# A scratch write of 256 columns on GpSimd ahead of each scatter in the experts' stage

## The chip, the cores and the metric

The kernel runs on one core of a Trainium2 chip. The metric is the device time of one execution in microseconds, the median of several runs; lower is better. The engines are named as the profile names them: PE is TensorE (PEld its weight loads), ACT is ScalarE, DVE is VectorE, POOL is GpSimd, SP is SyncE, which here only issues DMAs.

## What is computed

The input is 16 sequences of 512 tokens with 128 features. The first half is causal attention with 16 heads and ALiBi slopes, the second a mixture of 8 experts with the best 2 for each token, plus one shared expert. Each half ends with a residual sum and a layer norm. Cut to what matters here:

```python
x = layernorm(x + attention(x))                      # 8192 tokens x 128
logits = xf @ gate_w.T                               # 8 experts
probs = softmax(logits)
topw, topi = top_k(probs, 2)
topw = topw / (topw.sum(-1, keepdims=True) + 1e-20)
shared = (silu(xf @ shared_gate.T) * (xf @ shared_up.T)) @ shared_down.T
for e in range(8):                                   # hidden size 352
    y = (silu(xf @ gate[e].T) * (xf @ up[e].T)) @ down[e].T
    routed += y * comb[:, e]                         # comb: topw at topi, else 0
x = layernorm(x + shared + routed)
```

## The kernel before

The attention stage takes the first 790 us or so and is not touched. It leaves the normalised tokens in SBUF as `x1` (64 tiles of 128 tokens, each with an extra column for the token's number), the logits, and for each token the two places that it has in an order sorted by expert.

The experts' stage works on 64 tiles of 128 tokens in two chunks of 32 (`CHUNKS`, `CT`). For each chunk there is a DRAM buffer `x_sorted`, in which each token stands twice, under each of its experts, with groups padded to whole tiles: 72 tiles of 128 rows (`CSLOT`), 144 in all (`NSLOT`). The rows get there by **scatters of x**, one indirect DMA on GpSimd for each tile and choice (64 for a chunk, the helper `scatter`, line 336). Each sorted tile is loaded back by SyncE (`xs`, line 1219), transposed by TensorE (line 1299), multiplied with one expert's gate and up matrices (line 1277), passed through SiLU on ScalarE (line 1368) and the product on VectorE (line 1145), transposed again (line 1326), multiplied with the down matrix (line 1338), and copied by ScalarE from PSUM into one of four slots of `ys` (line 1393; the profile names the tile `e_raw`, as it lies in the space of the raw weights). From there a **scatter of y** on GpSimd (line 1432) writes it back in token order to the DRAM buffer `y_tokens`. Before ScalarE fills a slot of `ys` again, it waits until the scatter of four tiles back has landed (line 1390). Rows that only pad a group are left out by the bounds check.

The order of the work is a list of steps, written out by every engine: 24 steps of the shared expert on groups of four tiles (three steps a group, one for each part of the hidden size), 144 steps with one routed tile each, and 24 more of the shared expert. Each engine walks through the same steps and does its part, with fixed lags: at a step, TensorE does gate and up for the step's tile, the transpose of x for two steps ahead, that of the hidden tile for two back, and the down matrix for three back.

GpSimd's part of a step, in order, is this:

- At the first step of a shared group: the low part of the group's input (`group_x`, line 1420), for which TensorE waits before the group's gate two steps later (line 1267).
- At steps 10 to 23: one scatter of x for the second chunk (`scatter_next`), after a wait for the gate of the next step; two at every fourth step. That makes 18.
- At steps with a routed tile three back: the waits for the tile (`y_taken`) and for its row numbers (`row_ready`), then the scatter of y. In the first chunk `scatter_next` follows at 7 tiles of 10 (`PACE`), until the 64 scatters of x of the second chunk are done; the last of them follows the scatter of the 66th tile of y.
- The final norm: the inverse deviation as a power (`rstd`, line 1442) and the normalised tile (line 1447). For the first chunk's 32 tiles this comes at every second step of the second chunk (GpSimd's share at steps 104 to 166), for the second chunk's at every step from 175 on.

SyncE loads the first sorted tile of the second chunk only when all scatters of x have landed, and the first tile of `y_tokens` only when all of the chunk's scatters of y have landed; the loads of later tiles stand behind these waits in its queue.

Of the kernel before, what the change touches and what calls it, by code (L numbers as in the profile page):

```python
# [15 lines left out]
P = 128  # L16
# [317 lines left out]
def scatter(pool, keep, dram, c, t, n, done):  # L334

    pool.indirect_dma_start(out=dram["x_sorted"][c],
                            out_offset=bass.IndirectOffsetOnAxis(ap=keep["place_i"][n][:, c * CT + t:c * CT + t + 1], axis=0),
                            in_=keep["x1"][:, c * CT + t, :], in_offset=None).then_inc(done, 16)
# [626 lines left out]
STEPS = range(-LOAD, len(KINDS) - DOWN + NORM_LAG + 14)  # L965
MIX = ((PARTED + CSLOT + 4, 2), (PARTED + NSLOT + 5, 1))
SPLIT_AT = 8
PACE = 7


def tile_at(at):

    return (KINDS[at], WHICH[at]) if 0 <= at < len(KINDS) else (None, None)


def part_at(at, parts):

    kind, n = tile_at(at)
    if kind != SHARED:
        return None, None  # L980
    group, part = divmod(n, NCH)
    return (group, part) if part in parts else (None, None)


def mixed_at(step, lag):

    for chunk, (first, every) in enumerate(MIX):
        turn, rest = divmod(step - first, every)
        if rest == 0 and 0 <= turn - lag < CT:
            return chunk * CT + turn - lag  # L990
    return None


def experts(nc, io, dram, keep):

    with ExitStack() as ctx:
        def sb(name, shape, dt=F32):
            return ctx.enter_context(nc.sbuf_tensor("e_" + name, shape, dt))

        def ps(name):  # L1000
            return ctx.enter_context(nc.psum_tensor("e_" + name, [P, T], F32))

        def sem(name):
            return ctx.enter_context(nc.semaphore("e_" + name))
# [35 lines left out]
        var_eps = sb("var_eps", [P, TURN])  # L1040
        minus_half = sb("minus_half", [P, 1])
        rstd = sb("rstd", [P, TURN])

        gate_ps = [ps(f"gate_ps{n}") for n in range(2)]
        up_ps = [ps(f"up_ps{n}") for n in range(2)]
# [4 lines left out]
        names = """const_loaded experts_loaded const_set weight_kept weight_rest routed chosen prefix_ps prefix_kept placed places  # L1050
            exponents exponents_done weighted experts_set ids_set x_scattered row_ready x_ready xT_kept xT_rest gate_ready up_ready
            silu_done hid_done h_ready hT_kept y_ready y_taken half_set mix_half mixed stats_taken aggregated stats_ready
            rstd_ready result_ready group_kept group_rest group_ready group_taken""".split()
        S = {n: sem(n) for n in names}
        group_loaded = [sem(f"group_loaded{n}") for n in range(2)]
        xs_loaded = [sem(f"xs_loaded{n}") for n in range(TURN)]
# [6 lines left out]
        def split_at(step):  # L1063

            return divmod(step - SPLIT_AT, 2) if 0 <= step - SPLIT_AT < 2 * NE else None

        with nc.Block() as block:
# [327 lines left out]
            @block.gpsimd  # L1395
            def _(pool):
                pool.memset(minus_half[:], -0.5).then_inc(S["half_set"], 1)
                pool.wait_ge(S["half_set"], 1)
                scattered = [0]

                def scatter_next():

                    choice, t = divmod(scattered[0], CT)
                    if choice == 2:
                        return
                    if t == 0:
                        if choice == 0:
                            pool.wait_ge(S["places"], 1)
                        else:
                            pool.wait_ge(S["x_scattered"], 16 * CT)  # L1410
                        pool.tensor_copy(x1[:, CT:NTILE, C:RW], keep["ids"][:, choice, CT:NTILE].unsqueeze(2)).then_inc(S["ids_set"], 1)
                        pool.wait_ge(S["ids_set"], choice + 1)
                    scatter(pool, keep, dram, 1, t, choice, S["x_scattered"])
                    scattered[0] += 1

                for step in STEPS:
                    group, part = part_at(step + TURNED, (0,))
                    if group is not None:
                        pool.wait_ge(S["group_kept"], group + 1)
                        pool.tensor_tensor(group_x[group % 2][:, 1, :], group_in[group % 2][:],  # L1420
                                           group_x[group % 2][:, 0, :].bitcast(F32), ALU.subtract).then_inc(S["group_rest"], 1)
                    if 10 <= step < PARTED:
                        pool.wait_ge(S["gate_ready"], step + 1)
                        scatter_next()
                        if step % 4 == 3:
                            scatter_next()
                    kind, n = tile_at(step + DOWN)
                    if kind == ROUTED:
                        chunk, slot = n // CSLOT, n % TURN
                        pool.wait_ge(S["y_taken"], n + 1)  # L1430
                        pool.wait_ge(S["row_ready"], n + 1)
                        pool.indirect_dma_start(out=dram["y_tokens"][chunk],  # L1432
                                                out_offset=bass.IndirectOffsetOnAxis(ap=row_i[:, n:n + 1], axis=0),
                                                in_=ys[:, slot, :], in_offset=None, bounds_check=2 * CT * P - 1,
                                                oob_is_err=False).then_inc(y_stored[chunk][slot], 16)
                        if chunk == 0 and (n + 1) * PACE // 10 > n * PACE // 10:
                            scatter_next()
                    tile = mixed_at(step, 2)
                    if tile is not None:
                        slot = tile % TURN  # L1440
                        pool.wait_ge(S["stats_ready"], tile + 1)
                        pool.tensor_tensor(rstd[:, slot:slot + 1], var_eps[:, slot:slot + 1], minus_half[:],  # L1442
                                           ALU.pow).then_inc(S["rstd_ready"], 1)
                        if tile >= TURN:
                            pool.wait_ge(out_stored[slot], 16 * (tile // TURN))
                        pool.wait_ge(S["rstd_ready"], tile + 1)
                        pool.tensor_scalar(result[:, slot, :], mixed[:, slot, :], mean_var[:, slot, 0:1],  # L1447
                                           rstd[:, slot:slot + 1], ALU.subtract, ALU.mult).then_inc(S["result_ready"], 1)
# [30 lines left out]
def build(nc, io):  # L1479

    dram = {"out": io["out"],
            "x_sorted": [nc.dram_tensor(f"x_sorted{c}", (CSLOT * P, RW), F32).ap() for c in range(CHUNKS)],
            "x1T": nc.dram_tensor("x1T_all", (B, P, T), F32).ap(),
            "y_tokens": [nc.dram_tensor(f"y_tokens{c}", (2 * CT * P, C), F32).ap() for c in range(CHUNKS)]}
    with ExitStack() as ctx:
        def sb(name, shape, dt=F32):
            return ctx.enter_context(nc.sbuf_tensor(name, shape, dt))

        keep = {"x1": sb("x1_all", [P, NTILE, RW]), "logits": sb("logits", [P, NTILE, NE]), "rank": sb("rank", [P, NE]),
                "ids": sb("ids", [P, 2, NTILE]), "before": sb("before", [P, P], BF16), "onesb": sb("onesb", [P, P], BF16),  # L1490
                "top": [sb("best", [P, NTILE]), sb("second", [P, NTILE])], "keyed": sb("keyed", [P, CT, NE]),
                "top_key": sb("top_key", [P, CT]), "one": [sb(f"one{n}", [P, CT, NE]) for n in range(2)],
                "others": sb("others", [P, CT, NE]), "chosen": sb("chosen", [P, CT, NE], BF16),
                "counts": sb("counts", [P, NE, CT]), "running": sb("running", [P, NE, CT]),
                "ones_f": sb("ones_f", [P, NE * CT]), "first": sb("first", [P, NE]), "group_n": sb("group_n", [P, NE]),
                "group_i": sb("group_i", [P, NE], I32), "padded": sb("padded", [P, NE]), "shift": sb("place_shift", [P, NE]),
                "ends": sb("ends", [P, CHUNKS, NE]), "place": sb("place", [P, CT, NE]), "place_f": sb("place_f", [P, CT]),
                "place_i": [sb("place_best", [P, NTILE], I32), sb("place_second", [P, NTILE], I32)]}
        keep |= {"shared_in": sb("shared_in", [P, 2, F]), "shared_down": sb("shared_down", [P, NCH, C])}
        attention(nc, io, dram, keep)  # L1500
        experts(nc, io, dram, keep)
# [14 lines left out]
```

## Time and profile before

| | |
|---|---|
| median of 3 timed runs | 1244.45 us (1243.96 to 1244.94) |
| profiled execution, first to last instruction | 1288.1 us; the page has no other time for it |
| TensorE busy | 1067.3 us, 83% |
| VectorE, ScalarE, GpSimd busy | 829.4, 695.8, 703.8 us |
| attention | about 0 to 790 us |
| first shared stage (steps 0 to 23) | about 790 to 831 us |
| first chunk (72 tiles) | about 831 to 1037 us |
| second chunk (72 tiles) | about 1037 to 1199 us |
| second shared stage, then the last results | 1199 to 1254, then to 1288 us |

The profile is one execution of the program, taken by the hardware profiler. A timeline row has the start, the length, engine, line, operation, output and inputs; in square brackets stands how long the engine had been idle before, and what released it. "issue" there is time in which the engine waited for nothing that the profile shows, "remote" an unknown releaser. The time of a DMA instruction on GpSimd is that of writing its descriptors; the data move later.

### The profile page before, as it was taken

Reading aid. Unit: us, or ns where it says so; the run is one execution under the profiler, and the core shown is the slowest. Engines: PE = TensorE matmul, PEld = TensorE weight load, DVE = VectorE, ACT = ScalarE, POOL = GpSimd, SP = SyncE. Lnnn points to the kernel's source line nnn. Section 1 sums busy time; section 2 is a strip of 40 time slices with the busy share of each in tenths; the row PEclk is TensorE's granted clock in tenths of the full one; section 3 lists DMA queues with packets and bytes.
Section 4 is the critical chain, followed back from the end, with each engine's and each line's share of the span. In section 5 each row is a group of like instructions: output and inputs, shape, how many; then the busy total and the mean of one; then the engine's idle time right before and its main releaser. Section 6 shows DMA issues by size and latency. Waiting matters only on the chain. (4 is left out here: it accounts for less than half of the span.)

```text
span 1288.1 us, 28760 instructions
## 1 busy us (share of the span) xinstructions
PE 1067.3 (83%) x9396; PEld 725.3 (56%) x9396; DVE 829.4 (64%) x2134; ACT 695.8 (54%) x1513; POOL 703.8 (55%) x1166
## 2 busy tenths in 40 slices
PE   1677898898989988999888849988878879999990
PEld 0333444444444443444444328877777779999880
DVE  2667888898888988988887137732222226655594
ACT  1016666666666664766667714454444446666430
POOL 0004554454545543777677722655555537888686
PEclk9958999999999998999999858999999889999995
DMA  5624534344344442553341224222222123333242
GB/s 93 75 40 68 82 65 77 79 70 82 68 77 84 69 77 46 88 109 88 75 107 27 69 62 171 60 60 61 62 60 59 52 56 104 113 108 106 76 120 73
DMA packets 124769, 100.48 MB, mean 78 GB/s; under 512 B 19952, under 2 KB 115574, under 8 KB 124178
## 3 DMA queue, kind: packets, MB, share of 16 engines
q1 hardware_dynamic: 114786, 76.55, 29.6%
q0 software_dynamic: 8704, 16.87, 4.1%
q10 hardware_dynamic: 1136, 5.23, 1.2%
q8 instruction: 81, 1.33, 0.4%
q14 instruction: 62, 0.51, 0.2%
HBM read 37.88 MB, written 35.79 MB: 57 GB/s over the span
## 5 line engine op out<-in xcount | busy, mean ns | idle before, releaser
L709 ACT ACTIVATE probs<-scores 128x512 f32<-128x512 f32 x640 | 346.7, 599 | 112.5 <-PE scores L622 105.4
L772 POOL TENSOR_SCALAR_AFFINE_SELECT probs<-probs 128x256 f32<-128x256 f32 (+1 forms) x640 | 234.5, 380 | 248.6 <-ACT probs L709 238.5
L599 PE MATMUL maxed<-kstack,qstack 52*128 52x128 bf16 (+3 forms) x1152 | 223.2, 299 | 71.0 <-DMA kstack<-parts 38.3
L622 PE MATMUL scores<-qstack,kstack 64*128 64x512 bf16 (+3 forms) x1024 | 236.1, 304 | 40.9 <-ACT probs L709 17.4
L1145 DVE TENSOR_TENSOR e_hid<-e_gate,e_up_ps 128x352 f32<-128x352 f32 (+2 forms) x192 | 107.6, 561 | 234.5 <-ACT e_gate L1368 149.1
L919 DVE TENSOR_REDUCE maxA<-maxed 128x4 f32<-128x512 f32 x256 | 165.6, 684 | 81.1 <-PE maxed L606 80.4
L1432 POOL DMA_INDIRECT y_tokens<-e_raw,e_row_i x144 | 145.6, 1011 | 120.2 <-ACT e_raw L1393 81.2
L638 PE MATMUL pv<-probs,vaug 128*32 128x512 f32 (+3 forms) x2048 | 197.7, 460 | 2.9 <-POOL probs L772 2.9
L919 DVE TENSOR_REDUCE maxB<-maxed 128x4 f32<-128x512 f32 x256 | 162.4, 682 | 4.9 <-PE maxed L606 4.9
L604 PE MATMUL maxed<-causal,halves 64*128 64x256 bf16 (+1 forms) x640 | 159.7, 261 | 0.0
L622 PEld LDWEIGHTS scores<-qstack,kstack 64*128 64x128 bf16 x1024 | 75.7, 94 | 145.8 <-ACT probs L709 81.5
L1368 ACT ACTIVATE e_gate<-e_gate_ps 128x352 f32<-128x352 f32 (+2 forms) x192 | 95.5, 498 | 98.4 <-PE e_gate_ps L1267 57.9
L606 PE MATMUL maxed<-causal,halves 64*128 64x192 bf16 (+1 forms) x640 | 143.6, 228 | 0.0
L1338 PE MATMUL e_y_ps<-e_w_down,e_hT 128*128 (+1 forms) x864 | 128.0, 286 | 15.8 <-ACT e_raw L1393 13.0
L599 PEld LDWEIGHTS maxed<-kstack,qstack 52*128 52x128 bf16 x1152 | 74.8, 95 | 91.4 <-issue 41.0
L1338 PEld LDWEIGHTS e_y_ps<-e_w_down,e_hT 128*128 128x128 f32 (+1 forms) x864 | 112.8, 199 | 21.5 <-issue 21.2
L1277 PE MATMUL e_gate_ps<-e_w_in,e_xT 128*128 x432 | 108.9, 361 | 1.8 <-DVE e_w_in L1078 1.8
L1277 PE MATMUL e_up_ps<-e_w_in,e_xT 128*128 x432 | 96.0, 332 | 0.0
L1326 PE MATMUL e_h_ps<-e_ident,e_hid 128*128 128x128 f32 x432 | 73.9, 282 | 20.3 <-ACT e_hT L1380 14.7
L1380 ACT ACTIVATE e_hT<-e_h_ps 128x384 f32<-128x384 f32 x144 | 71.0, 493 | 24.5 <-PE e_h_ps L1326 17.6
L919 DVE TENSOR_REDUCE maxC<-maxed 128x4 f32<-128x512 f32 x128 | 82.5, 684 | 1.0 <-PE maxed L606 0.4
L1277 PEld LDWEIGHTS e_up_ps<-e_w_in,e_xT 128*128 128x128 f32 x432 | 76.6, 195 | 0.0
(160 smaller groups left out, 1824.1 us busy)
## 6 DMA issues: line engine op xcount, KB each, us to landing
qstack<-parts SPq DMA_DIRECT2D x192, 64.0 KB
kstack<-parts SPq DMA_DIRECT2D x192, 64.0 KB
x_sorted<-zeros SPq DMA_DIRECT2D x16, 580.5 KB
e_xs<-x_sorted SPq DMA_DIRECT2D x144, 64.5 KB
e_raw<-y_tokens SPq DMA_DIRECT2D x64, 128.0 KB
xin<-in_x SPq DMA_DIRECT2D x16, 256.0 KB, 3.1
xres<-in_x SPq DMA_DIRECT2D x16, 256.0 KB
x1T_all<-ynT SPq DMA_DIRECT2D x16, 256.0 KB
```

The source lines that it names most:

```text
L599: pe.matmul(bank[:, at:at + (k1 - k0) * P], q[rows, slot, i * P:(i + 1) * P], ks[rows, slot, k0 * P:k1 * P], start=first, stop=False, skip ...
L604: pe.matmul(bank[:, at:at + wide], halves[rows, 0, :], causal[rows, 0:wide], start=False, stop=False, skip_group_check=True)
L606: pe.matmul(bank[:, at + ROWS:at + wide], halves[rows, 1, :], causal[rows, 2 * P:P + ROWS + wide], start=False, stop=True, skip_group_chec ...
L622: last = pe.matmul(scores[st.at(0, SEQ_UNITS, n) % SB][:, col:col + width], ks[rows, slot, kt * P:(kt + 1) * P], q[rows, slot, kt * P:T], ...
L638: last = pe.matmul(pv[hh * VW:(hh + 1) * VW, kt * P:T], vaug[st.par(off)][:, kt, g * QUAD + hh, :], probs[g % 2][:, at * T + col:at * T + ...
L709: act.activation(probs[g % 2][:, u * T:(u + 1) * T], scores[st.at(0, SEQ_UNITS, UNITS * g + u) % SB][:], ACT.Exp).then_inc(S["exp_done"], 1)
L772: pool.affine_select(out=view, in_=view, compare_op=ALU.is_ge, fill=0.0, base=0, pattern=pattern, channel_multiplier=-1).then_inc(S["maske ...
L919: dve.tensor_reduce(out.rearrange("p a b -> p (a b)"), maxed[st.at(max_stage(n), MAXB, n) % MB][:].rearrange("p (j t) -> p j t", t=P), AX. ...
L1145: dve.tensor_tensor(hid[step % len(hid)][rows, 0:cols], gate[step % 2][rows, 0:cols], up_ps[step % 2][rows, 0:cols], ALU.mult).then_inc(S[ ...
L1277: last = pe.matmul(bank[:, 0:F], xT[n % len(xT)][:, x_part, :], w_in[:, e, w, w_part, :].rearrange("p a f -> p (a f)"), start=m == 0, stop ...
L1338: last = pe.matmul(y_ps[:, 0:C], hT[n % 2][0:fw, j * P:(j + 1) * P], w_down[0:fw, e, j, :].rearrange("p a c -> p (a c)"), start=j == 0, st ...
L1432: pool.indirect_dma_start(out=dram["y_tokens"][chunk], out_offset=bass.IndirectOffsetOnAxis(ap=row_i[:, n:n + 1], axis=0), in_=ys[:, slot, ...
```

## The change

A tile `pause` of 128 partitions x 256 float is added and a semaphore `paused`. A helper writes zeros into the tile, with a wait for the write before, and is called ahead of every scatter of x in this stage and ahead of the two waits of every scatter of y. Nothing reads the tile. The scatters of x for the first chunk, which run in the attention stage, stay as they are.

```diff
+PAUSE = 256
...
+        pause = sb("pause", [P, PAUSE])
...
-                scattered = [0]
+                scattered, pauses = [0], [0]
+
+                def take_pause():
+
+                    if pauses[0]:
+                        pool.wait_ge(S["paused"], pauses[0])
+                    pool.memset(pause[:], 0.0).then_inc(S["paused"], 1)
+                    pauses[0] += 1
...
                         pool.wait_ge(S["ids_set"], choice + 1)
+                    take_pause()
                     scatter(pool, keep, dram, 1, t, choice, S["x_scattered"])
                     scattered[0] += 1
...
                     if kind == ROUTED:
                         chunk, slot = n // CSLOT, n % TURN
+                        take_pause()
                         pool.wait_ge(S["y_taken"], n + 1)
                         pool.wait_ge(S["row_ready"], n + 1)
                         pool.indirect_dma_start(out=dram["y_tokens"][chunk],
```

## Rows read from the trace of the kernel before

**Rows 1.** The head of the profile's page.

```profile
span 1288.1 us, 28760 instructions
```

**Rows 2.** Stage table: busy us (instructions) of each engine, clock, DMA share, GB/s.

```profile
801.00:832.00 31.00, 29.20 (x181) 25.16 (x180) 26.50 (x48) 14.57 (x31) 23.79 (x23) 1.00 0.23 65
840.50:1032.80 192.30, 155.65 (x1056) 144.24 (x1054) 52.61 (x198) 91.00 (x263) 108.96 (x112) 0.95 0.21 60
1068.00:1197.00 129.00, 129.00 (x988) 127.07 (x987) 76.82 (x331) 88.79 (x247) 107.50 (x124) 1.00 0.38 107
```

**Rows 3.** Groups by form on POOL: busy us, mean ns, idle us before, releasers.

```profile
L738 POOL MEMSET ones_f<- 128x256 f32 x1 | 0.3, 317 | 0.0
```

**Rows 4.** Timeline of POOL in the first chunk: start us, us, instruction, idle before.

```profile
840.57 1.00 POOL L1432 DMA_INDIRECT y_tokens<-e_raw,e_row_i  x1 [9.10 <-ACT e_raw L1393]
...
947.52 0.98 POOL L1432 DMA_INDIRECT y_tokens<-e_raw,e_row_i  x1 [1.88 <-ACT e_raw L1393]
948.81 0.97 POOL L336 DMA_INDIRECT x_sorted<-x_all,place_second  x1 [0.31 <-issue]
950.08 0.99 POOL L1432 DMA_INDIRECT y_tokens<-e_raw,e_row_i  x1 [0.30 <-issue]
951.37 0.96 POOL L336 DMA_INDIRECT x_sorted<-x_all,place_second  x1 [0.30 <-issue]
...
1032.83 0.96 POOL L336 DMA_INDIRECT x_sorted<-x_all,place_second  x1 [0.30 <-issue]
```

**Rows 5.** Timeline of PE and ACT in the first chunk and at its end.

```profile
953.99 0.27 PE L1299 MATMUL e_x_ps<-e_ident,e_xs 128*128 128x128 f32 x1
...
956.17 0.28 ACT L1372 ACTIVATE e_xT<-e_x_ps 128x128 fp32r<-128x128 f32 x1 [2.39 <-remote]
...
1036.97 0.47 PE L1299 MATMUL e_x_ps<-e_ident,e_xs 128*128 128x128 f32 x1 [4.65 <-DMA e_xs<-x_sorted]
```

**Rows 6.** Waits from 840 to 1020 us: us in total, times, longest.

```profile
ACT e_raw L1393 <- remote: 25.9, 15, 2.2
ACT e_raw L1393 <- PE e_y_ps L1338: 12.0, 28, 1.4
```

**Rows 7.** Waits from 1060 to 1200 us.

```profile
ACT e_raw L1393 <- PE e_y_ps L1338: 14.4, 38, 0.9
```

**Rows 8.** Timeline of POOL in the second chunk.

```profile
1068.95 0.61 POOL L1442 TENSOR_TENSOR e_rstd<-e_var_eps,e_minus_half 128x1 f32<-128x1 f32 x1
...
1173.05 0.98 POOL L1432 DMA_INDIRECT y_tokens<-e_raw,e_row_i  x1 [0.30 <-issue]
1174.04 0.60 POOL L1442 TENSOR_TENSOR e_rstd<-e_var_eps,e_minus_half 128x1 f32<-128x1 f32 x1
1174.82 0.80 POOL L1447 TENSOR_SCALAR e_raw<-e_raw,e_mean_var,e_rstd 128x128 f32<-128x128 f32 x1 [0.18 <-POOL e_rstd L1442]
1175.80 1.10 POOL L1432 DMA_INDIRECT y_tokens<-e_raw,e_row_i  x1 [0.18 <-issue]
1177.20 0.99 POOL L1432 DMA_INDIRECT y_tokens<-e_raw,e_row_i  x1 [0.30 <-issue]
...
1197.70 1.28 POOL L1420 TENSOR_TENSOR e_group_x<-e_group_in,e_group_x 128x512 fp32r<-128x512 f32 x1
```

**Rows 9.** Timeline of POOL and PE in the first shared stage.

```profile
807.39 1.30 POOL L1420 TENSOR_TENSOR e_group_x<-e_group_in,e_group_x 128x512 fp32r<-128x512 f32 x1
808.85 1.09 POOL L336 DMA_INDIRECT x_sorted<-x_all,place_best  x1 [0.17 <-issue]
...
808.94 0.94 PE L1267 MATMUL e_gate_ps<-e_group_x,e_w_in 128*128 128x512 f32 x3
...
815.78 0.94 PE L1267 MATMUL e_gate_ps<-e_group_x,e_w_in 128*128 128x512 f32 x3
```

**Rows 10.** Timeline of PE at the start of the second shared stage.

```profile
1199.13 0.93 PE L1267 MATMUL e_gate_ps<-e_group_x,e_w_in 128*128 128x512 f32 x3 [0.54 <-POOL e_group_x L1420]
```

More of the change, by code:

```diff
@@ L1052, in experts @@
             silu_done hid_done h_ready hT_kept y_ready y_taken half_set mix_half mixed stats_taken aggregated stats_ready
-            rstd_ready result_ready group_kept group_rest group_ready group_taken""".split()
+            rstd_ready result_ready paused group_kept group_rest group_ready group_taken""".split()
         S = {n: sem(n) for n in names}
```

## The prediction, made before the change was run

> **What bounds the kernel now.** I read the page first, for the span and the busy shares, then the stage table, then the groups of GpSimd by form, then GpSimd's own timeline in two stages, and last the waits. No engine bounds the whole: the span is 1288.1 us [rows 1], and the change touches only the last third, where TensorE is busy 29.2 of 31, then 155.65 of 192.3, then all of 129 us [rows 2]. What matters there is GpSimd, although it is busy only 57% of the long middle stretch.
>
> A scatter costs GpSimd more than its bar. Where scatters queue up, one starts 1.29 us after the y scatter at 947.52 and the next 1.27 us after that [rows 4]: 0.97 to 0.99 us of work and 0.30 us in which it is idle on "issue". Behind a computing instruction the gap is 0.18 us and the bar 1.10 us [rows 8], or 1.09 us for a scatter of x [rows 9]: again 1.28 us from the end of what came before. So 1.28 us is the price of a scatter, and none of it overlaps the instruction ahead of it.
>
> In the first routed chunk GpSimd has 66 scatters of y and 46 of x between 840.57 and 1032.83 us [rows 4], 112 in all and 111 intervals, 192.3 us. At 1.28 us they need 142.1 us; TensorE, at 128.75 us for 62 tiles in the second chunk [rows 8], would need 65 x 2.08 = 135 us. Neither explains 192.3. The other 50 us are stalls of this kind: TensorE's transpose into e_x_ps starts at 953.99 and is 0.27 us long, ScalarE's copy of it waits for nothing else by the code, and starts at 956.17, after 2.39 us of idle time that the trace puts down to "remote" [rows 5]. There are 15 such waits ahead of e_raw alone, 25.9 us together [rows 6]. The one shown comes a few microseconds behind the scatters of rows 4, which follow each other at 1.28 us. In the second chunk, where a scatter comes every 2.08 us on average, e_raw waits for TensorE's own matmul, 0.9 us at most [rows 7].
>
> In the second chunk GpSimd is full. Two tiles cost it two scatters, the power (rstd) and the normalised tile: from the rstd at 1068.95 to the subtraction for group 8 at 1197.70 there are 31 such pairs of steps in 128.75 us, 4.15 us each [rows 8], and by price 2 x 1.28 + 0.61 + 0.18 + 0.80 = 4.15 us. TensorE already waits 0.54 us for that subtraction [rows 10]. GpSimd has no slack in this stage.
>
> **How profile and median stand.** The sum is to be made against the profiled execution, whose span alone is 1288.1 us; the median of three timed runs is 1244.45 us, 43.65 us less. So something in the profiled execution takes longer than in a timed one. The one thing in the trace that has this size and no cause in the code is the 50.2 us of stalls just worked out. Without them the span would be 1288.1 - 50.2 = 1237.9 us, and 6.5 us around it make the median. I take it that the stalls belong to the recording. The Trainium skill's page "Runtime: NRT & Kernel Launch", section "The ~15µs preamble/postamble breakdown", has a profile's total some 6.2 us above the time reported without one; by it 37.5 us of the difference would be left over, so this case does not fit that figure. The page "NOTIFIC — the notification-queue block", section 7.1, says that its internal pipeline holds back the producer rather than lose a record, which would be a way for recording to slow TensorE; no run here shows it yet.
>
> **The change part by part.** It adds 208 pauses (64 ahead of scatters of x in this stage, 144 ahead of those of y), each a memset of 128 x 256 float on GpSimd, and a semaphore. The trace of before has that very shape once: 0.317 us [rows 3]. A pause starts about 0.01 us behind a scatter (rstd does, at 1174.04 [rows 8]), and puts the scatter behind it into the form that follows a computing instruction: 0.01 + 0.32 + 0.18 + 1.10 = 1.61 us instead of 1.28, so 0.33 us more. The wait on the pause before is for an instruction that lies a whole scatter back: nothing. Bounds: below, 0.20 us, if scatter and memset overlapped by the 0.12 us in which the two gaps differ (0.30 and 0.18); above, 0.43 us, if the 0.11 us by which the bar grows came on top. I take 0.33, because the sums of gap and bar agree in rows 8 and 9.
>
> Shared stage, 18 pauses. GpSimd's subtraction for a group runs 807.39 to 808.69, and TensorE starts the group's gate at 808.94 [rows 9]: 0.25 us of cover. Four scatters stand between two subtractions; with pauses such a turn is 4 x 1.61 + 1.45 = 7.9 us against the 6.84 us from one group's gate to the next (808.94 to 815.78). The first shown slips by 0.6 us behind TensorE, the next by about 1.0 more, then there are only three scatters and it recovers. Together +1.6 us, 0 to 3.
>
> First chunk, 65 tiles with 46 scatters of x. The pause stands ahead of the wait for e_raw, so where GpSimd waits for a tile it is hidden: the waits before scatters are over 1 us at both ends of the stage, and 9.1 us before the first [rows 4]. Further in, GpSimd has 1.7 x 1.61 = 2.74 us of work per tile against TensorE's 2.08, so it falls behind at once, and with four slots of ys ScalarE soon waits for the stores and all go at GpSimd's pace: 111 x 1.60 = 177.6 us. Against a timed run without the stalls (142.1) this is +35.5 us. Against the profile (192.3) it is -14.7. What is late next is the same in both: TensorE's transpose of the second chunk's first tile waits for the last scatter of x and its load, from 1032.83 to 1036.97 [rows 4, 5], and this tail of 4.1 us stays.
>
> Second chunk. GpSimd's pair of steps goes from 4.15 to 4.15 + 2 x 0.335 = 4.82 us against TensorE's 4.16. Queued behind each pause are the scatter, the rstd, the result and in the end the subtraction for group 8, for which TensorE waits already. 31 x 0.67 = +20.8 us, all of it on the path; the four slots can only delay when it is seen. Behind that subtraction four scatters remain (1.3 us at most if nothing covered them), at the pace of the shared tiles, and the last 32 results have no scatters; I count nothing.
>
> The sum for a timed run: 1244.45 + 1.6 + 35.5 + 20.8 = 1302.4 us. For the profiled execution: 1288.1 + 1.6 - 14.7 + 20.8 = 1295.8 us, if the pauses, which set scatters 1.6 us apart, also end the stalls.
>
> **The rivals.**
> The stalls are real. Then timed runs have them too, and the change takes them away as in the profile: 1244.45 + 1.6 - 14.7 + 20.8 = 1252.2 us. For it: nothing in the trace marks the stalls as the recorder's. Against it: the 43.65 us would then have to lie elsewhere, and I find no place for them. Half of them real would give about 1277.
>
> The pauses win. The stalls are real and a pause costs less than I take. In the first chunk the gain is 50.2 us less 111 pauses, in the second the loss is 62 pauses; with some 5 in the shared stage that count, the balance is zero at 50.2 / 178 = 0.28 us a pause. At the lower bound of 0.20 us it is -50.2 + 22.2 + 12.4 + 1.0 = -14.6, that is 1229.8 us. Against it: rows 8 and 9 leave no room for an overlap, and the memset's bar alone is 0.317.
>
> No slack, but less of it than I think. If a scatter takes less time in an unrecorded run, say 1.20 us, TensorE bounds both stages before the change, and part of the pauses is covered: 111 x 1.52 - 135 = +34 and 31 x (4.64 - 4.16) = +15, with 1 us for the shared stage 1294 us. This, and 0.43 us a pause on the other side (+76 us, 1320), are the ends of my forecast's own range; I narrow it to 1288 to 1310.
>
> The pauses are hidden everywhere, or are not carried out: 1244 us. It needs GpSimd to have 0.33 us to spare per scatter in an unrecorded run, that is a scatter under 0.95 us, less than the bar alone.
>
> **How the numbers follow.** My forecast has 0.66, half of the stalls real 0.08, all of them real 0.16, the pauses win 0.07, hidden 0.03. The predicted time is the likeliest's, 1302. The range of 8 in 10 has to take in the case of the real stalls: 1249 to 1310, with 1288 to 1310 for the forecast alone. What a measurement of this kernel can tell from no change is about 0.2%, 2.5 us. Faster by more than that: 0.08 (the winning pauses and a little of the real stalls); within it: 0.03; slower by more: 0.89.
>
> **What would show it.** In the profile of the changed kernel: memsets of 0.32 us with a 0.18 us gap behind them; scatters in the first chunk 1.60 us apart and never at 1.28; idle time of ScalarE on "remote" gone, and "DMA y_tokens" in its place as ScalarE waits for a slot; the pairs in the second chunk 4.8 us long with TensorE idle for some 0.3 us a tile; a span of about 1296 us. If the time is then above the span, or just under it, the stalls were the recorder's; if the time is some 40 us under the span as before, the missing time lies elsewhere and the first rival holds. I would be wrong if GpSimd's pair in the second chunk stayed under 4.3 us, or if scatters at 1.6 us still left ScalarE on "remote".

## The result, and the profile after

The changed kernel takes 1284.72 us (median of 4 runs, 1279.14 to 1287.53), the kernel before 1244.2 us (4 runs, 1239.36 to 1244.94, among them the three known before). The ratio is 1.0325, 95% interval 1.0292 to 1.0358: 40.5 us slower. I had forecast 57.9 us slower. The ratios and intervals here and below are those of the comparison as recorded; they leave the slow executions out and are not exactly the quotients of the medians beside them.

First the head of the page of the changed kernel, and the pauses from its groups by form.

```profile
span 1285.8 us, 28982 instructions
...
PE 1071.4 (83%) x9396; PEld 725.5 (56%) x9396; DVE 834.5 (65%) x2134; ACT 695.4 (54%) x1513; POOL 768.5 (60%) x1374
...
L1407 POOL MEMSET e_pause<- 128x256 f32 x208 | 69.7, 335 | 0.3
```

All 208 pauses are there. This span is 2.3 us *below* that of rows 1, although the kernel takes 40.5 us more, and that was the first thing to clear up. This profiled execution has a time beside it, 1287.53 us, 1.7 us above its span. For the profile before the page gave none.

Now the stage table (stretch, its length, busy us of PE, PEld, DVE, ACT and POOL, then clock, DMA share, GB/s): first chunk from the first to the last scatter of its burst (192.3 us in rows 2), then the second chunk from the first rstd to the subtraction for group 8 (129.0 us in rows 2).

```profile
850.50:1016.30 165.80, 145.34 (x1055) 139.08 (x1053) 52.21 (x199) 91.70 (x264) 145.10 (x223) 0.98 0.25 69
1051.90:1193.00 141.10, 134.09 (x990) 129.03 (x988) 76.90 (x329) 89.04 (x248) 125.03 (x185) 0.99 0.35 98
```

The timeline of POOL in the changed kernel: the ends of the first chunk and four neighbours inside it.

```profile
850.50 1.00 POOL L1443 DMA_INDIRECT y_tokens<-e_raw,e_row_i  x1 [7.54 <-ACT e_raw L1395]
...
943.50 0.34 POOL L1407 MEMSET e_pause<- 128x256 f32 x1
944.00 0.96 POOL L336 DMA_INDIRECT x_sorted<-x_all,place_second  x1 [0.17 <-issue]
944.95 0.34 POOL L1407 MEMSET e_pause<- 128x256 f32 x1
945.46 0.99 POOL L1443 DMA_INDIRECT y_tokens<-e_raw,e_row_i  x1 [0.17 <-issue]
...
1016.34 0.96 POOL L336 DMA_INDIRECT x_sorted<-x_all,place_second  x1 [0.17 <-issue]
```

The scatters at 944.00 and 945.46 are 1.46 us apart, where I had said 1.60 and where two in rows 4 are 1.27 to 1.29 apart. What ScalarE's copy waits for in this stretch is now a slot of `ys` (rows 6 had "remote" there):

```profile
ACT e_raw L1395 <- DMA y_tokens<-e_raw,e_row_i: 46.7, 37, 4.0
...
ACT e_raw L1395 <- PE e_y_ps L1340: 6.7, 29, 0.9
```

And the chain of waits that ended last, for some microseconds of the first chunk (start, us, and what the time went to; a DMA's time ends with its landing):

```profile
946.44 0.33 POOL e_pause L1407
946.93 0.96 POOL x_sorted L336
947.89 0.33 POOL e_pause L1407
948.22 0.17 issue
948.39 3.45 DMA y_tokens<-e_raw,e_row_i
...
951.92 0.29 ACT e_raw L1395
```

The pauses stand on the chain itself; then comes a scatter of y with its landing, then ScalarE, which waited for that slot.

### The profile page after: what moved, and what is told of

Same layout as the page of the kernel before. It is cut to its first block and busy times, and to the rows that moved or that the text cites. A ratio compares the mean times of both kernels' runs of the same rounds, so it can differ in the third digit from the quotient of the medians.

```text
span 1285.8 us, 28982 instructions
## 1 busy us (share of the span) xinstructions
PE 1071.4 (83%) x9396; PEld 725.5 (56%) x9396; DVE 834.5 (65%) x2134; ACT 695.4 (54%) x1513; POOL 768.5 (60%) x1374
## 5 line engine op out<-in xcount | busy, mean ns | idle before, releaser
L599 PE MATMUL maxed<-kstack,qstack 52*128 52x128 bf16 (+3 forms) x1152 | 226.1, 301 | 71.7 <-DMA kstack<-parts 36.4
L622 PE MATMUL scores<-qstack,kstack 64*128 64x512 bf16 (+3 forms) x1024 | 238.9, 307 | 44.8 <-DMA qstack<-mparts 17.7
L1395 ACT ACTIVATE e_raw<-e_y_ps 128x128 f32<-128x128 f32 x144 | 39.9, 277 | 90.5 <-DMA y_tokens<-e_raw,e_row_i 68.9
L606 PEld LDWEIGHTS maxed<-causal,halves 64*128 64x128 bf16 x640 | 64.0, 101 | 25.8 <-issue 7.6
```

What stands on the lines that cost most here:

```text
L599: pe.matmul(bank[:, at:at + (k1 - k0) * P], q[rows, slot, i * P:(i + 1) * P], ks[rows, slot, k0 * P:k1 * P], start=first, stop=False, skip ...
L606: pe.matmul(bank[:, at + ROWS:at + wide], halves[rows, 1, :], causal[rows, 2 * P:P + ROWS + wide], start=False, stop=True, skip_group_chec ...
L622: last = pe.matmul(scores[st.at(0, SEQ_UNITS, n) % SB][:, col:col + width], ks[rows, slot, kt * P:(kt + 1) * P], q[rows, slot, kt * P:T], ...
```

## The experiments

Three questions were open: whether the 50 us of stalls belong to the recording, what one pause costs, and how the 40.5 us divide between the two chunks. Each comparison is with the kernel before on the same chip. To compare stages I read the same marks in every trace: first subtraction of group_x, first scatter of y, last scatter of x, transpose of the 73rd tile, first rstd, subtraction for group 8, end. The stretch ahead of the first mark, attention, which no edit touches, varies from 771 to 788 us from run to run, so I compare the others. The times in the second column are medians and the stages are those of one execution: the two kernels with the norm on VectorE were profiled in executions of 1290.65 and 1300.73 us, 10 and 14 us above their medians, with 788 us in attention. The stages do not all repeat equally well. With the same scatters and no pauses in it, the shared stage has 67.9 to 70.3 us, and the stretch to the first rstd 34.6 to 36.2, so a difference of 1 us or so in either means nothing (with pauses the latter has 35.5 to 37.2); the two chunks and the rest repeat within 0.5 us among kernels with the same pauses in them and no stalls.

| kernel (chip) | time, us | shared | first chunk | last scatter of x to first rstd | second chunk | rest |
|---|---|---|---|---|---|---|
| before, again (9) | 1248.32 | 69.3 | 143.5 | 34.6 | 128.2 | 90.4 |
| changed (no chip on record) | 1284.72 | 70.3 | 165.8 | 35.5 | 141.0 | 92.9 |
| second chunk only (9) | 1261.51 | 67.9 | 143.4 | 35.6 | 141.0 | 92.9 |
| first chunk only (9) | 1271.99 | 70.1 | 166.0 | 35.7 | 128.2 | 90.4 |
| one column (9) | 1249.37 | 69.9 | 145.5 | 36.4 | 128.6 | 90.4 |
| first chunk, 320 columns (8) | 1279.66 | 71.6 | 171.7 | 36.4 | 128.2 | 90.4 |
| 512 columns (15) | 1323.88 | 70.1 | 189.5 | 37.2 | 155.6 | 92.8 |
| changed, norm on VectorE (15) | 1281.18 | 70.3 | 179.2 | 36.0 | 127.3 | 87.8 |
| before, norm on VectorE (15) | 1286.74 | 70.3 | 189.5 | 36.2 | 127.3 | 87.8 |
| scatters earlier (15) | 1285.93 | 77.1 | 178.4 | 35.7 | 128.7 | 90.4 |
| scatters earlier (2) | 1241.20 | 69.3 | 136.5 | 36.8 | 128.2 | 90.2 |
| the profile of rows 1 to 10 | none given | 70.0 | 192.3 | 36.1 | 128.7 | 90.4 |

### The kernel before, unchanged

> The kernel before, unchanged, profiled and timed once more. Theory R (the stalls of ScalarE and TensorE in the first routed chunk belong to the recording): the profile again has a span near 1288 us and stalls of some 50 us between the first scatter of y and the last scatter of x (192 us long, scatters at 1.28 us in bursts), while the timed runs stay near 1244 us, so ratio 1.000. Theory S (the stalls are real and the first profile was of an odd execution, or the missing 44 us lie elsewhere): span and time agree to a few microseconds, or they differ again with the stretch no longer 192 us.

It took 1248.32 us (10 runs) against 1245.69 (19 runs), ratio 1.0018 (0.9980 to 1.0055). Its head, stage table and waits in the first chunk:

```profile
span 1246.8 us, 28760 instructions
...
850.20:993.70 143.50, 138.27 (x1055) 135.91 (x1053) 52.12 (x199) 97.03 (x264) 108.89 (x113) 1.00 0.29 80
1028.10:1156.30 128.20, 128.20 (x985) 126.90 (x984) 76.05 (x328) 93.08 (x247) 107.18 (x124) 1.00 0.38 108
...
ACT e_raw L1393 <- DMA y_tokens<-e_raw,e_row_i: 10.7, 12, 2.1
```

The same program, recorded in the same way, has no "remote" waits here; the first chunk takes 143.5 us instead of 192.3, and I had worked out 142.1 without stalls. This is what theory S had said of span and time, and recording by itself does not make the stalls. ScalarE already waits for slots in it, 10.7 us in all, with scatters 1.28 us apart:

```profile
911.56 0.99 POOL L1432 DMA_INDIRECT y_tokens<-e_raw,e_row_i  x1 [0.30 <-DVE e_row_i L1153]
912.85 0.96 POOL L336 DMA_INDIRECT x_sorted<-x_all,place_second  x1 [0.30 <-issue]
914.12 0.99 POOL L1432 DMA_INDIRECT y_tokens<-e_raw,e_row_i  x1 [0.30 <-ACT e_raw L1393]
```

### Each chunk alone

```diff
-                        take_pause()
+                        if chunk:
+                            take_pause()
```

In this kernel the pause in `scatter_next` is gone too. The other one keeps that and has `if not chunk`.

> Pauses only ahead of the 72 scatters of y of the second chunk. In the profile of the changed kernel the 31 pairs of steps there took 141.1 us instead of 128.75 us, and the end behind them 2.5 us more. Both theories: time up by 12 to 15 us, 1257 to 1259 us. Theory R: the profile still has the stalls in the first chunk (192 us), span near 1302 us. Had my price of 0.33 us a pause held, +20.8 us, 1265 us.

> Pauses only ahead of the 64 scatters of x in this stage and of the 72 scatters of y of the first chunk. Theory R: without a recording the first chunk goes at 1.28 us a scatter before (142 us for 111 intervals) and at 1.49 us now (165.8 us as profiled), so time up by 23.7 us plus 0 to 2, about 1268 to 1270 us, and the profile's span falls by some 26 us. Theory S: the time falls by 26 us, to 1218 us, as the profile's stretch does (192.3 to 165.8 us).

Second chunk alone: 1261.51 us, ratio 1.0144 (1.0074 to 1.0214), +15.8 us; I had expected 12 to 15, with the growth of the rest behind group 8 (92.9 against 90.4) counted in. First chunk alone: 1271.99 us, 1.0216 (1.0153 to 1.0279), +26.3 us, near the 23.7 to 25.7 expected, and not the fall by 26 us that stalls in the timed runs would have given. Together they are 42.1 us, against 40.5 for the whole change. Each interval is some 8 us to either side, so the sum alone says little; the stages say more: the first chunk, the second chunk and the rest have with their pauses the lengths that they have in the changed kernel, and without them those of the kernel before.

### One column, 320 and 512 columns

```diff
-PAUSE = 256
+PAUSE = 1
```

> The pause is a memset of one column instead of 256 (0.10 us instead of 0.33 us by the profile's rows). A scatter behind it would start 0.98 + 0.10 + 0.17 = 1.25 to 1.28 us after the one before, so no more than now. Theory that the price of a pause is the memset's length less the gap that it takes the place of (0.33 - 0.13): time 1244 +- 3 us, no change; the profile's stalls stay, since the scatters come as densely as before. If the price were that of an instruction more (my prediction's 0.33 us less 0.23, so 0.10 us a pause): 1244 + 111 x 0.10 + 62 x 0.10 = 1261 us.

1249.37 us (10 runs), ratio 1.0047 (1.0016 to 1.0079): a little more than the "no change" that I expected, and far from the 1261 us of a price for an instruction as such. The instruction and its semaphore, with almost no work, from POOL's timeline:

```profile
910.28 0.12 POOL L1407 MEMSET e_pause<- 128x1 f32 x1
910.59 0.99 POOL L1443 DMA_INDIRECT y_tokens<-e_raw,e_row_i  x1 [0.19 <-issue]
911.54 0.16 POOL L1407 MEMSET e_pause<- 128x1 f32 x1
911.88 0.96 POOL L336 DMA_INDIRECT x_sorted<-x_all,place_second  x1 [0.19 <-issue]
```

The scatters are 1.29 us apart, as without a pause: the memset lies where the 0.30 us gap was, and only 0.19 us of gap is left behind it. The first chunk is 2.0 us longer all the same, which I have not explained; the 1.9 us in the stretch to the first rstd are of the size by which that stretch varies.

The size alone, 320 columns (first chunk only) and 512 (everywhere):

> Pauses of 320 columns, only ahead of the scatters of x in this stage and of y in the first chunk: scatters 1.52 us apart (1.47 at 256 columns, 1.69 at 512). Theory T (a chip that stalls does so where scatters follow each other at 1.5 us or less): without stalls, first chunk 111 x 1.52 = 169 us, second as before, 128.7; on a stalling chip 1287 - 23 = 1264 us, faster than both kernels there; on a chip without stalls 1245 + 26 = 1271 us, slower. If the stalls went on at 1.52 us, first chunk near 180 us and 1276 us on the stalling chip.

> The pause has 512 columns. The memset should take 0.54 us (0.33 us for 256 columns, 0.14 for one: some 0.2 us for 256 more; or 0.22 by 0.208 for 129 and 0.317 for 256). Law from the first four runs: one scatter to the next takes 0.97 + memset + 0.17 - 0.02 us, so 1.67 to 1.69 us: first chunk 111 x 1.68 = 186 us instead of 165.8, second chunk pairs 4.55 + 0.43 = 4.98, 154 us instead of 141; time 1285 + 20 + 13 + 1 = 1319 us. If a pause had a fixed price of 0.2 us whatever its length, 1285 us.

320 columns: 1279.66 us, ratio 1.0276 (1.0196 to 1.0356), first chunk 171.7 us. I had expected less: 64 further columns cost the first chunk 5.7 us, and the shared stage is 1.4 us longer, which with 512 columns it is not. As the chip was one without stalls, the run says nothing about my theory of them. 512 columns: 1323.88 us, ratio 1.0267 (1.0199 to 1.0336), on a chip with stalls (below); 1319 us had been expected, for a chip without them. POOL's timeline with 320, then with 512:

```profile
943.74 0.39 POOL L1407 MEMSET e_pause<- 128x320 f32 x1
944.30 0.99 POOL L1444 DMA_INDIRECT y_tokens<-e_raw,e_row_i  x1 [0.17 <-issue]
945.26 0.41 POOL L1407 MEMSET e_pause<- 128x320 f32 x1
945.84 0.97 POOL L336 DMA_INDIRECT x_sorted<-x_all,place_second  x1 [0.17 <-issue]
```

```profile
942.53 0.54 POOL L1407 MEMSET e_pause<- 128x512 f32 x1
943.24 0.99 POOL L1443 DMA_INDIRECT y_tokens<-e_raw,e_row_i  x1 [0.17 <-issue]
944.20 0.57 POOL L1407 MEMSET e_pause<- 128x512 f32 x1
944.94 0.99 POOL L1443 DMA_INDIRECT y_tokens<-e_raw,e_row_i  x1 [0.17 <-issue]
```

So the distance of two scatters is 1.29, 1.46 to 1.47, 1.51 to 1.54 and 1.70 us with 1, 256, 320 and 512 columns. That is the memset, the gap of 0.17 us and the scatter of 0.97 us, less 0.02 to 0.03 us by which the memset's bar begins inside the scatter's: with 512 columns 0.57 + 0.17 + 0.97 - 0.02 = 1.69.

### The final norm moved to VectorE, with and without the pauses

If GpSimd alone bounds the second chunk, its 12.8 us must vanish when GpSimd loses the normalised tile (0.80 + 0.18 us a pair). The edit, made to the changed kernel and to the one before, cut to its core (the waits that go with it are left out here):

```diff
+                    done = mixed_at(step, NORM_LAG)
+                    if done is not None:
...
+                        dve.tensor_scalar(result[:, slot, :], mixed[:, slot, :], mean_var[:, slot, 0:1],
+                                          rstd[:, slot:slot + 1], ALU.subtract, ALU.mult).then_inc(S["result_ready"], 1)
...
-                        pool.tensor_scalar(result[:, slot, :], mixed[:, slot, :], mean_var[:, slot, 0:1],
-                                           rstd[:, slot:slot + 1], ALU.subtract, ALU.mult).then_inc(S["result_ready"], 1)
```

> The changed kernel, with the final norm's subtraction and product (0.80 us a tile on GpSimd, line 1458) moved to VectorE. Theory P (in the second chunk a pause costs because GpSimd's pair of steps, 4.55 us with pauses, is longer than TensorE's 4.16): the pair now needs 4.55 - 0.98 = 3.6 us, TensorE bounds the stage, and its 31 pairs go back from 141.0 to 128 to 129 us, the first chunk stays at 165.8 us; time 1285 - 13 - 2 = 1270 us, some microseconds less if the tail gains. Theory Q (the pauses cost by what they do to the scatters' own landing or to VectorE's port, not by GpSimd's time): the pairs stay near 141 us and the time near 1285 us.

> The kernel before (no pauses) with the same 0.80 us moved to VectorE. In the second chunk TensorE bounds at 4.16 us a pair, so GpSimd's relief gives nothing there; in the tail behind TensorE's last step some 14 tiles go at GpSimd's 1.54 us each, which becomes 0.6 us on GpSimd and whatever VectorE needs (about 1.2 us by its busy time of 16 us for the tail). Theory P: 1245 - 1 to - 5 us. If VectorE, which makes the product for TensorE in the same stage, becomes late: slower by up to 5 us.

The changed kernel with it took 1281.18 us, the one before with it 1286.74, and the kernel before on this chip 1287.49 us (27 runs, 1278.98 to 1303.15); ratios 0.9940 (0.9903 to 0.9978) and 0.9989 (0.9955 to 1.0024). My numbers had been written for a kernel before of 1246 us, so the times can't be held against them; the stages can. The second chunk in the stage table of the first of the two:

```profile
1074.00:1201.30 127.30, 127.30 (x978) 126.04 (x978) 84.47 (x359) 92.47 (x245) 98.55 (x154) 1.00 0.38 108
```

The second chunk is back to 127.3 us, with pauses as without, and TensorE is busy in all of it: the place of that loss is GpSimd's full pair of steps, and not what the pauses do to landings or to VectorE (theory Q). The chip was a surprise. The kernel before takes 1287.5 us there (median of 27 executions), what rows 1 show as a span. First the waits in the first chunk of the kernel before with the moved norm, then those of the changed one with it:

```profile
ACT e_raw L1401 <- remote: 23.6, 13, 2.4
```

```profile
ACT e_raw L1403 <- remote: 14.3, 16, 1.7
```

So on this chip the stalls are in the times, too, and not in one odd profile. At 1.47 us between scatters they cost less: the first chunk takes 179.2 us instead of 189.5, still 13 us above the 165.8 that the pauses alone need. With the norm moved, the kernel with pauses is thus the faster one there, by 5.6 us in the medians. With 512 columns, on the same chip, no "remote" is left in front of e_raw:

```profile
ACT e_raw L1395 <- DMA y_tokens<-e_raw,e_row_i: 70.2, 41, 3.8
...
ACT e_raw L1395 <- PE e_y_ps L1340: 5.3, 16, 0.9
ACT e_raw L1395 <- issue: 1.7, 9, 0.3
```

The first chunk's 189.5 us are nearly 111 x 1.70 = 188.7, the pace of GpSimd alone. That they equal the 189.5 us of the kernel with stalls is chance.

### The scatters of x earlier

If the first chunk is bound by GpSimd before the change, moving 7 of its scatters into the shared stage must shorten it to TensorE's pace.

```diff
-PACE = 7
+PACE = 6
...
-                        if step % 4 == 3:
+                        if step % 4 == 3 or step >= 20:
+                            scatter_next()
+                        if step == PARTED - 1:
+                            for _ in range(4):
+                                scatter_next()
```

> The kernel before (no pauses) with 7 of the scatters of x moved ahead, from the first chunk into the 9 us in which GpSimd waits for the first tile of y, and 6 instead of 7 tiles in 10 with a scatter behind them. GpSimd's work in the first chunk falls from 1.7 x 1.28 = 2.18 us a tile to 1.6 x 1.28 = 2.05, under TensorE's 2.08. Theory P (GpSimd's time per tile bounds the first chunk, before the change already): 143.5 us from the first scatter of y to the last of x becomes 135 to 137 us, time 1245 - 7 = 1238 us. If something else bounds it (the loads of xs, the landing of y): no change.

It was run first on the chip with stalls: 1285.93 us, ratio 0.9967 (0.9932 to 1.0002), inconclusive; the first chunk went to 178.4 us, but 7.1 us came back in the shared stage, and waits on "remote" remained. Then again:

> The kernel before with 7 scatters of x moved ahead of the first chunk and 6 instead of 7 tiles in 10 with a scatter, run before only on a stalling chip (0.997, interval up to 1.000). On a chip without stalls GpSimd's 1.28 us a scatter alone should bound the first chunk: 143.5 us become 135 to 137 us (TensorE's 2.08 us a tile), the shared stage gets 0 to 7 us longer (7 us on the stalling chip, where the moved scatters made the first tile of y wait). Theory P: faster by 0 to 7 us, 0.995 to 1.000 of the kernel before. On a stalling chip again 0.997.

1241.20 us (12 runs) against 1245.64 (17 runs), ratio 0.9971 (0.9943 to 0.9999). Stage table of the first chunk:

```profile
848.38:984.88 136.50, 136.50 (x1051) 135.17 (x1050) 51.61 (x198) 98.90 (x262) 100.98 (x105) 1.00 0.30 80
```

TensorE is busy without a break, at 136.5 us (I had worked out 135 for its pace), where the kernel before has 138.27 of 143.5. GpSimd's 111 intervals do bound the first chunk of the kernel before. Of the 7.0 us between 143.5 and 136.5 only 4.8 are gained: the last scatter of x here follows the 65th tile of y and not the 66th, and 2.2 us come back in the next column (36.8 against 34.6). The medians differ by 4.4 us. This version is 0.3% faster than the kernel before, at the edge of what the runs can tell; the changed one is, by its own comparison, 3.2% slower.

### The changed kernel twice more

> The changed kernel once more, beside the kernel before on the same chip. The last four kernels ran on a chip on which the kernel before takes 1287 us, the ones before them on a chip on which it takes 1246 us. Theory C (the 45 to 50 us of stalls in the first chunk are real, but only some chips have them): on a chip with the stalls the first chunk takes some 179 us (as in the run with the norm on VectorE and pauses of 256 columns) instead of 192, the second 141 instead of 128.7, so the change costs -13 + 12.5 + 2.5 = +2 to +9 us there, 1290 to 1296 us beside 1287; on a chip without them 165.8 and 141 us, 1285 us beside 1245, as measured first. Theory R (the stalls come with the recording of one execution): 1285 us on any chip.

> The changed kernel beside the kernel before, for a comparison on a chip that stalls. Theory C (stalls are real, on some chips only): where the kernel before takes 1287 us, the first chunk takes some 179 us instead of 190 to 192 and the second 141 instead of 128.7, time 1290 to 1296 us, +0.2 to +0.7%; where it takes 1243 to 1246 us, 1284 us as twice before. Theory R (the stalls come with the recording): 1284 us on either.

1284.05 us against 1242.92 (7 runs), ratio 1.0305 (1.0234 to 1.0377), and 1280.99 against 1241.66 (7 runs), ratio 1.0283 (1.0204 to 1.0362). Both were meant for the chip with stalls and ran on others (8 and 0), without stalls. They repeat the result: first chunk 165.9 and 166.3 us, second 141.3 and 141.2.

## Why the prediction was right and where it failed

**The direction and the places were right.** The pauses land on two stages that GpSimd bounds. The same marks in the traces, changed against before without stalls, give +22.3 us in the first chunk, +12.8 in the second, +2.5 behind it, +1.0 in the shared stage and +1.0 between the chunks: 39.6 us of the 40.5. The first three stand clear of what these stages vary by and are shown part by part by the two kernels with half of the pauses and by the moved norm. The last two do not: my +1.6 us for the shared stage is neither confirmed nor refuted, and with 512 columns that stage has 70.1 us, no more than without pauses.

**The mis-sized term is the price of a pause**: 0.33 us by my sum, 0.19 measured. The step that was wrong is "puts the scatter behind it into the form that follows a computing instruction: 0.01 + 0.32 + 0.18 + 1.10". The gap did become 0.17, but the scatter kept its 0.97. Two neighbouring pauses of the second chunk of the changed kernel, on POOL's timeline, show what the 1.10 goes by:

```profile
1139.99 0.80 POOL L1458 TENSOR_SCALAR e_raw<-e_raw,e_mean_var,e_rstd 128x128 f32<-128x128 f32 x1 [0.18 <-POOL e_rstd L1453]
1140.74 0.30 POOL L1407 MEMSET e_pause<- 128x256 f32 x1
1141.23 1.10 POOL L1443 DMA_INDIRECT y_tokens<-e_raw,e_row_i  x1 [0.18 <-issue]
1142.33 0.33 POOL L1407 MEMSET e_pause<- 128x256 f32 x1
1142.82 0.98 POOL L1443 DMA_INDIRECT y_tokens<-e_raw,e_row_i  x1 [0.17 <-issue]
1143.81 0.60 POOL L1453 TENSOR_TENSOR e_rstd<-e_var_eps,e_minus_half 128x1 f32<-128x1 f32 x1
```

Both scatters stand behind the same kind of memset. Only the first, with the rstd and the normalised tile since the scatter before it, is 1.10 us long. So a memset does not lengthen the next scatter, and it lies in the gap of 0.30 us of which only 0.17 has to follow it: 0.13 us of every pause is free. The measured 0.19 us lies just below my lower bound of 0.20 us, which had counted such an overlap; I had set it aside and taken the sum from rows 8 and 9, where the instruction ahead is a tensor operation, and not a memset. In the first chunk 111 x (1.47 - 1.28) = 21 us instead of 35.5; in the second a pair takes 141.0 / 31 = 4.55 us, 0.41 us more than 128.2 / 31, instead of 0.67. With the measured lengths of the three stages in it my sum is 1244.45 + 1.0 + 22.3 + 12.8 = 1280.6 us. The forecast's own range, 1288 to 1310, missed the time for this reason. The wide one, 1249 to 1310, has it, but it was stretched so far down for a rival, the real stalls, that was not what happened: that the time lies in it is luck.

**Behind group 8 I had counted nothing, and it costs 2.5 us.** (Five scatters of y stand there, and not the four that I counted.) The timeline of PE in the changed kernel:

```profile
1194.32 1.62 PE L1269 MATMUL e_gate_ps<-e_group_x,e_w_in 128*128 128x512 f32 x3 [4.28 <-POOL e_group_x L1430]
...
1201.81 0.95 PE L1269 MATMUL e_gate_ps<-e_group_x,e_w_in 128*96 128x512 f32 x3
```

and its stage table just there (stretch, us, busy of each engine, clock, DMA share, GB/s):

```profile
1194.30:1200.20 5.90, 5.88 (x19) 4.95 (x20) 0.69 (x1) 1.36 (x3) 4.18 (x7) 0.50 0.23 65
1200.20:1206.00 5.80, 5.80 (x38) 5.00 (x37) 1.37 (x2) 2.92 (x7) 3.85 (x5) 1.00 0.02 3
```

TensorE, busy without a break in the 4 us before, waits 4.28 us for GpSimd's subtraction (0.54 in rows 10). Its granted clock is 0.50 (1.2 of 2.4 GHz) for the next 5.9 us and 1.00 after, and the first gate takes 1.62 us where rows 10 have 0.93. A half clock over 5.9 busy us is some 2.9 us of lost work, about what this stage lost. The other traces leave no room for the pauses behind group 8 as the cause. In all five with pauses in the second chunk and the norm on GpSimd, TensorE waits 4.2 to 6.3 us there, its clock is 0.50 for a few microseconds, and the rest takes 92.8 to 93.1 us. With the norm on VectorE the same pauses stand behind group 8, but TensorE does not wait:

```profile
1202.62 0.95 PE L1277 MATMUL e_gate_ps<-e_group_x,e_w_in 128*128 128x512 f32 x3
```

Its clock stays at 1.00, and the rest takes 87.8 us with pauses as without. I looked at who waits for a late subtraction, and not at what the wait does to the engine that waited.

**The stalls: number right, reason wrong.** I put the 43.65 us between the first profile and its median down to the recording. The timed runs were indeed free of the stalls, and 1288.1 - 50.2 = 1237.9 us is near what the same program then shows (1246.8, of which attention took 10 us more: 780.9 against 770.6). But the same program recorded on chip 9 has no stalls, so the recording as such is not the reason. On chip 15 the kernel before takes 1287.5 us, on chips 0, 2, 8 and 9 it takes 1241.7 to 1245.7. All runs on chip 15 were made at one time, so the chip and the occasion can't be told apart. That the first profile was taken under the one condition and the timed runs under the other fits both, but no chip is given for either, so it is inferred.

The traces hold one thing more that I had overlooked. In the four profiles of chip 15, and in that of rows 1 to 10, about a fifth of the semaphore updates are missing (18407 to 19472 of them stand there, 22958 to 23412 in the nine others), with 512 columns, too, where no stalls are left. So the recording did run differently there. As every execution on chip 15 has a span and a granted clock on record, none is known to have run without any recording, and that recording slows TensorE on that chip alone is not excluded. What is refuted is what I had written, that the stalls come with any recording.

"6.5 us around it" failed as well: every profile with a time has it 1.7 us above its span, so my sign for the recorder's guilt, a time at or above the span, would have come up whatever the cause. The Trainium skill's 6.2 us ("Runtime: NRT & Kernel Launch", "The ~15µs preamble/postamble breakdown") is not seen either: the profiled execution here, 1287.53 us, lies among the timed ones. And no run shows the recorder holding back TensorE, for which I had named the Trainium skill's page "NOTIFIC — the notification-queue block", section 7.1: the profile of the kernel before on chip 9 is free of it, and for chip 15 it stays open.

The rivals. "The stalls are real" was therefore right about the chip and wrong about these timed runs. Whether the changed kernel wins where stalls exist was not measured, as it met that chip only with the norm moved. An estimate from the table, from the changed kernel with the moved norm: 1281.18 + 13.7 for the second chunk + 5.1 for the rest = 1300.0 us against 1287.5. Another, from the kernel before there: 1287.5 - 10.3 for the first chunk + 12.3 for the second + 2.5 for the rest = 1292 us. By both, the 10 us that the first chunk gains are less than the other stages lose. The mechanism of "the pauses win" is thus seen (179.2 us against 189.5), its result is not. "Hidden everywhere" fell with the second chunk, where GpSimd has no slack; "less slack" supposed scatters that take less time in unrecorded runs. Nothing shows them, as the stages of the profiles give 39.6 of the 40.5 us between the medians; a run known to be unrecorded, which would settle it, is not there.

**Of the signs named in advance**: memsets of 0.34 us (0.32 said) with 0.17 behind them, yes; "DMA y_tokens" in place of "remote", yes, though it had gone already in the kernel before on such a chip; pairs of 4.8 us, no, 4.55; TensorE idle for some 0.3 us a tile there, no, 0.11 (134.09 busy of 141.1 us, for 62 tiles); a span of 1296 us, no, 1285.8, by the price. The pair is above 4.3 us, the limit that I had set for being wrong.

**What stays open** is what delays the work on chip 15, and why only there. The trace's semaphore records, as far as they are there, say where: in the profile of before the transpose at 953.99 (rows 5) ends at 954.26, but its increment arrives at 956.15, just ahead of ScalarE's copy at 956.17, while increments by ScalarE, VectorE and GpSimd arrive within 0.01 us. In the first chunk 159 of 291 recorded increments of TensorE are more than 0.1 us late in that profile, 163 of 269 at 1.47 us between scatters (at most 3.9 us late, where 5.2 was the most at 1.28), and none of 247 at 1.70 us; on chip 9 none of 328 at 1.28. So at 1.47 us they are not fewer, only less late. That goes together in three spacings on one chip and is not shown as a cause; no run varied it further.

## What to carry to other kernels

Price an inserted instruction by a row in which the same kind of instruction stands in the same place; a gap on "issue" ahead of a DMA is partly room in which a short instruction is free, and the form "behind a computing instruction" need not hold for a memset. When a profile and the median differ by some per cent, profile the kernel before again, on another chip if there is one, before a cause is named: one look took out a theory worth 50 us. Count the records, too: a trace that lacks many was taken under other conditions. And a delay on a busy TensorE can have a second price, the clock that it comes back with.

## What the runs showed of the hardware

- An indirect scatter of 128 rows of 512 bytes (516 for those of x) takes GpSimd 0.96 to 0.99 us and 0.30 us of gap. The bar is 1.10 us when the rstd and the normalised tile ran since the last one, and a memset alone does not lengthen it. A memset of n columns ahead of it costs about 0.00, 0.19, 0.24 and 0.41 us for 1, 256, 320 and 512 columns of float.
- Chip 15 and chips 0, 2, 8 and 9 ran the same program some 3.5% apart (1287.5 against 1241.7 to 1245.7 us). In the profiles nearly all of the difference lies in the stage where scatters come 1.28 us apart for long, and those of chip 15 lack about a fifth of the semaphore updates.
- With a wait of 4.28 us TensorE's granted clock fell to 0.50, where it stayed for 5.9 us of work; after 0.56 us of waiting, in the kernel before, it was 1.00.
